# The normalised x of a gated layer: its scaling on ScalarE in place of GpSimd, in four slots of each chunk

## The chip, the cores and the metric

The kernel runs on one core of a Trainium2 chip. The metric is the device time of one execution in microseconds; what is compared is the median of several executions. The engines are named as the profile names them: PE is TensorE (matmuls), PEld its weight loads, DVE is VectorE, ACT is ScalarE, POOL is GpSimd, SP the engine that issues the DMAs.

## What is computed

x has the shape 4 x 2048 x 512. Each row is normalised to xn; one branch is a linear recurrence over the 2048 steps (q, k, v, a 128 x 128 memory M), the other a quantised feed-forward layer on the rows of xn with its own normalisation inside; the second, through a silu, gates the first.

```python
xn = (x - mean(x)) / sqrt(var(x) + 1e-5)

q, k, v = xn @ Wq.T, xn @ Wk.T, xn @ Wv.T
M_new = 0.99 * M + v_t.T @ k_t / b ;  r_t = q_t @ M.T
s = (r @ Wo.T) * sigmoid(gate)

h = (xn - mean(xn)) * rsqrt(var(xn) + 1e-5) * ln_gamma + ln_beta
y = silu(h @ dequant(fc1_q, fc1_scales) + fc1_bias)        # 512 -> 2048
z = y @ dequant(fc2_q, fc2_scales) + fc2_bias              # 2048 -> 512
g = silu(xn + 0.5 * z)
out = x + s * g
```

The change concerns the xn in `xn + 0.5 * z`: it is made again from x, late in the work on a chunk, as x times a scale of its row plus a shift of its row.

## The kernel before

The 2048 steps are cut into 16 chunks of 128 steps; with a batch of 4 that is four tiles of 128 rows by 512 columns a chunk (i from 0 to 3). Every engine runs the same hand-written loop of slots, 64 a chunk and 36 more at the end; what an engine does in slot e of a chunk is fixed by tables of slot numbers at the head of the file, and inside a slot by the order of the `if` lines in that engine's loop. Each engine works its own list strictly in order; semaphores tie the lists together.

In each slot TensorE does one step of fc1 (two matmuls of 128x512, L491) and one step of fc2 (two more, L509), and in some slots a side job of the recurrence: kv in slots 1, 13, 25, 37, q in slot 3, and for each tile kt, scores, read and wo at 4, 7, 11 and 14 slots after its kv, and a transposition (`turn`) in slots 52, 54, 57 and 60. The fc1 sum of a block J of 128 columns is built in four steps g, two slots apart. After each of the first three ScalarE multiplies the PSUM bank by a ratio (`rescale`, L638), and the next step waits for that; after the fourth it makes the silu (L645), and the first step of block J + 2, which uses the same bank, waits for that. Two blocks are worked in turn, so a rescale or silu of slot G is waited for by TensorE in slot G + 2, for the silus of even blocks as well. VectorE then splits y into two halves of 16 bits (`y_high` L760, `y_low` L765), which fc2 reads some slots later, and rescales the fc2 sum after each step (L774).

ScalarE also does the copies of the recurrence out of PSUM: `kv_copy` L610, `q_copy` L602, `kt_copy` L616, `r_copy` L621, `s_copy` L632, and, behind each `turn`, `g_high` L584 and `h_whole` L593. GpSimd splits h (L1073, L1077), makes the row statistics (L1038 to L1061) and normalises the next chunk's tiles (L1021).

A chunk is finished while the next one runs. In slots 8 to 11 of the next chunk VectorE puts z of the four tiles into `z_rows` (L779). GpSimd has made xn ready for it: `prepare` in slots 0, 3, 15 and 18 (`PREPARE_AT`) multiplies x by the row's scale and adds its shift (L1103), into one of the two buffers of `xz`, and then adds half of the fc2 bias to it in place (L1106). `add_z` in slots 13, 14, 17 and 20 (`ADD_AT`) adds it to `z_rows` (L1111). ScalarE makes the silu of that, `gate_silu` in slots 17, 19, 21 and 29 (`GATE_AT`, L664), and GpSimd multiplies by s and adds x, `output` in slots 18, 22, 26 and 30 (`OUT_AT`, L1117, L1120); SP stores the tile and loads the next x into its row of `x_again`. As `xz` has two buffers, the pieces for tiles 2 and 3 wait for the `add_z` of tiles 0 and 1. The last chunk is finished in the tail; its four `prepare` steps stand in its own slots 44, 46, 48 and 50 (`LAST_PREPARE_AT`) and write to `g_rows`, which is free then.

In the first chunk ScalarE uses the `xz` buffers for another purpose: it widens the fc2 weights there (`q2_widen`, L656), an activation with a scale and a shift from SBUF to SBUF.

Of the kernel before, what the change touches and what calls it, by code (L numbers as in the profile page):

```python
# [10 lines left out]
ALU = mybir.AluOpType  # L11
ACT = mybir.ActivationFunctionType
# [18 lines left out]
STEPS = 64  # L31
# [8 lines left out]
Q_AT = 3  # L40

Q_LAG, K_LAG, V_LAG, KT_LAG, R_LAG, S_LAG, GHIGH_LAG, HFULL_LAG = 1, 1, 2, 1, 1, 1, 1, 2
GATE_AT = (17, 19, 21, 29)

STATS_AT, MOMENTS_AT = (0, 1, 2, 3), (5, 6)
FIRST_STATS_AT, FIRST_MOMENTS_AT = (18, 20, 22, 24), (26, 27)
# [1 line left out]

HSPLIT_LAG = 3
NORMALISE_AT = (36, 38, 40, 42)  # L50
PREPARE_AT, ROWS_AT, FIRST_ROWS_AT = (0, 3, 15, 18), 7, 28

LAST_PREPARE_AT = (44, 46, 48, 50)
ADD_AT, OUT_AT = (13, 14, 17, 20), (18, 22, 26, 30)

Q1_AT = tuple(3 + 3 * n for n in range(FB // 2))
RATIO2_AT, TOP_Q2_AT, Q2_SCALE_AT = 6, (0, 1, 3, 5), 8
# [15 lines left out]
def build(nc, x, wqkv, wo, gate, m0, q1, q2, b2, params, out):  # L73
# [27 lines left out]
    def finishing(G, at, last_at):  # L101

        c, e = divmod(G, STEPS)
        if c == NCH:
            at = last_at
        return (c - 1, at.index(e)) if c > 0 and e in at else None

    def fc1_step(G):

        start = G if G % 2 == 0 else G - 5  # L110
        if start < 0:
            return None
        J, g = 2 * (start // 8) + G % 2, start % 8 // 2
        return (J, g) if J < NJ else None
# [20 lines left out]
    with ctx:  # L135
# [435 lines left out]
        def _(act):  # L571
# [16 lines left out]
            def h_whole(c, k, bank):  # L588
                if c == 0:
                    act.wait_ge(h_scales, 1)  # L590
                    act.wait_ge(turn_done, k + 1)
                wait(act, h_done, 4 * c + k - 1)
                act.activation(h_full[:, k % 2, :], bank[:], ACT.Identity,  # L593
                               bias=beta_s[:, k:k + 1], scale=gamma_s[:, k:k + 1]).then_inc(h_full_done, 1)
# [53 lines left out]
            def q2_widen(n):  # L648
# [4 lines left out]
                if n % 4 == 0:  # L653
# [2 lines left out]
                act.activation(wide[:, n % 2, :], q2_in_sb[:, n, :], ACT.Identity, bias=q2_shift[:, 0:1],  # L656
                               scale=up_q2).then_inc(q2_wide, 1)

            def gate_silu(c, i):
                if c < NCH - 1:  # L660
                    act.wait_ge(z_sum, NT * c + i + 1)
                else:
                    act.wait_ge(z_sum_last, i + 1)
                act.activation(z_rows[:, i, :], z_rows[:, i, :], ACT.Silu).then_inc(z_silu, 1)  # L664
# [31 lines left out]
            act.wait_ge(s1_scaled, 1)  # L696

            for G in range(SLOTS):
                if at := fc1_step(G):
                    if at[1] < KC - 1:  # L700
                        rescale(*at)
                    else:
                        silu(at[0])
                if G in Q1_AT:
                    if G == Q1_AT[0]:
                        act.wait_ge(q1_ready, 1)
                    q1_piece(FB // 2 + Q1_AT.index(G), up_q1, q1_shift[:, 0:1])
                if G in Q2_AT:
                    q2_widen(Q2_AT.index(G))
                if at := job_behind(G, Q_LAG, "q"):  # L710
                    q_copy(*at, side[JOB_BANK[G - Q_LAG]])
                if at := job_behind(G, K_LAG, "kv"):
                    kv_copy(*at, 0, side[JOB_BANK[G - K_LAG]])
                if at := job_behind(G, V_LAG, "kv"):
                    kv_copy(*at, 1, side[JOB_BANK[G - V_LAG]])
                if at := job_behind(G, KT_LAG, "kt"):
                    kt_copy(*at, side[JOB_BANK[G - KT_LAG]])
                if at := job_behind(G, R_LAG, "read"):
                    r_copy(*at, side[JOB_BANK[G - R_LAG]])
                if at := job_behind(G, S_LAG, "wo"):  # L720
                    s_copy(*at, side[JOB_BANK[G - S_LAG]])
                if at := job_behind(G, GHIGH_LAG, "turn"):
                    g_high(*at, side[JOB_BANK[G - GHIGH_LAG]])
                if at := job_behind(G, HFULL_LAG, "turn"):
                    h_whole(*at, side[JOB_BANK[G - HFULL_LAG]])
                if at := finishing(G, GATE_AT, LAST_GATE_AT):
                    gate_silu(*at)

# [279 lines left out]
        def _(pool):  # L1008
# [75 lines left out]

            def prepare(c, i):

                n = NT * c + i
                if c == 0 and i == 0:
                    pool.wait_ge(b2_halved, 1)
                if i == 0:  # L1090
                    pool.wait_ge(rows_done, c + 1)
                pool.wait_ge(x_again_in[i], 64 * (c + 1))
                to = xz[:, i % 2, :]
                if c == NCH - 1:
                    to = last_xz[:, i, :]
                    if i == 0:

                        pool.wait_ge(turn_done, KC * NCH)
                elif i >= 2:
                    pool.wait_ge(z_sum, NT * c + i - 1)  # L1100
                elif c > 0:
                    pool.wait_ge(z_sum, NT * (c - 1) + i + 3)
                pool.tensor_scalar(to, x_again[:, i, :], rs[:, c % 3, i:i + 1], nmr[:, c % 3, i:i + 1],  # L1103
                                   ALU.mult, ALU.add).then_inc(xz_scaled, 1)
                pool.wait_ge(xz_scaled, n + 1)
                pool.tensor_tensor(to, to, b2_half[:], ALU.add).then_inc(xz_done, 1)  # L1106

            def add_z(c, i):
# [96 lines left out]
```

## Time and profile before

| what | value |
|---|---|
| runs | 1252.54 us median of 3 (1252.32 to 1252.96) |
| the profiled execution | 1252.95 us, of which 1251.1 us are its span |
| granted TensorE clock, mean | 0.989 of full speed (2.4 GHz) |
| busy PE, DVE, ACT, POOL | 95%, 90%, 73%, 57% of the span |
| busy PEld | 49% of the span |
| chain that ended last | PE 78%, DVE 16%, issue 3%, ACT 1%, POOL 1% |

A row of the timeline has the start, the duration, engine, line and operation, what is written and read, and the count where neighbours were merged; in brackets stands the idle time of the engine before it, where there was any worth noting, and what ended it. Two neighbours on an engine may overlap: an instruction can be issued while the one before it still drains, so the distance from start to start is shorter than the duration. The middle chunk of the trace from which most rows are taken starts its slot 0 on TensorE at 562.53 us and its slot 16 at 584.53 us.

### The profile page before, as it was taken

How to read it: one execution, taken by the hardware profiler on the slowest of the kernel's cores; microseconds unless marked ns; L12 is line 12 of the kernel's file. 1: busy time of each engine (PE TensorE's matmuls, PEld its weight loads, DVE VectorE, ACT ScalarE, POOL GpSimd, SP SyncE). 2: the span in 40 equal slices, each digit the busy share in tenths (PEclk: the TensorE clock that was granted, in tenths of full speed). 3: DMA queues.
4: the chain of work that ended last, by engine and by line, in shares of the span. 5: the costliest groups of instructions: out<-in, count | busy, mean ns of one | idle time of the engine just before them, and what ended most of it. 6: DMA issues, size and time to landing. Idle time of an engine off the chain costs nothing.

```text
span 1251.1 us, 18966 instructions
## 1 busy us (share of the span) xinstructions
PE 1186.3 (95%) x6028; PEld 616.0 (49%) x6028; DVE 1124.8 (90%) x1965; ACT 913.8 (73%) x1590; POOL 711.4 (57%) x796
## 2 busy tenths in 40 slices
PE   2789999999999999999999999999999999999994
PEld 1344554545455554555555455454545545454551
DVE  7799899899998989999898989999898998999887
ACT  6588677777767777786777777777776777778673
POOL 6056737649273673927467383755837376492742
PEclk9799999999999999999999999999999999999997
DMA  9511030402103040120303113030210304020011
GB/s 332 178 42 34 20 83 1 102 1 57 45 9 94 1 102 1 43 60 1 102 1 81 22 30 73 1 101 1 67 35 18 85 1 101 1 55 13 24 46 35
DMA packets 41620, 65.68 MB, mean 52 GB/s; under 512 B 11696, under 2 KB 11952, under 8 KB 41008
## 3 DMA queue, kind: packets, MB, share of 16 engines
q1 hardware_dynamic: 41232, 64.36, 19.3%
q8 instruction: 51, 0.84, 0.3%
q14 instruction: 49, 0.40, 0.1%
q10 hardware_dynamic: 288, 0.08, 0.0%
HBM read 47.59 MB, written 16.81 MB: 51 GB/s over the span
## 4 chain that ended last, share of the span: by engine, by line
PE 78%; DVE 16%; issue 3%; ACT 1%; POOL 1%; DMA 1%; SPq 0%; DVEq 0%; ACTq 0%
PE blk L491 29%; PE blk L509 29%; PE side L451 7%; DVE blk L774 6%; PE side L476 4%; PE side L440 3%; DVE g_lo L744 3%; DVE y_split L765 2%; DVE y_split L760 2%; DVE tops L812 1%; PE side L469 1%; PE side L470 1%; PE side L468 1%; PE side L461 1%; PE side L427 1%
## 5 line engine op out<-in xcount | busy, mean ns | idle before, releaser
L774 DVE TENSOR_TENSOR blk<-blk,ratio_rows 128x512 f32<-128x512 f32 x960 | 649.3, 692 | 108.7 <-PE blk L509 97.9
L638 ACT ACTIVATE blk<-blk,ratio 128x512 f32<-128x512 f32 x768 | 508.2, 670 | 249.8 <-PE blk L491 240.2
L509 PE MATMUL blk<-w_sb,y_split 128*128 128x512 f16 x2048 | 609.0, 379 | 10.9 <-DVE y_split L765 8.1
L491 PE MATMUL blk<-h_split,q_sb 128*128 128x512 f16 x2048 | 612.8, 381 | 5.1 <-ACT blk L638 3.1
L509 PEld LDWEIGHTS blk<-w_sb,y_split 128*128 128x128 f16 x2048 | 197.1, 98 | 262.6 <-DVE blk L774 20.3
L491 PEld LDWEIGHTS blk<-h_split,q_sb 128*128 128x128 f16 x2048 | 192.9, 98 | 218.1 <-issue 36.8
L645 ACT ACTIVATE y_full<-blk,par,last 128x512 f32<-128x512 f32 x256 | 201.8, 788 | 55.0 <-PE blk L491 54.5
L1073 POOL CAST h_split<-h_full 128x512 f16<-128x512 f32 x64 | 41.0, 641 | 320.1 <-ACT h_full L593 320.0
L765 DVE SCALAR_TENSOR_TENSOR y_split<-y_full,up,y_split 128x512 f16<-128x512 f32 x256 | 214.8, 839 | 0.0
L760 DVE TENSOR_SCALAR y_split<-y_full,up 128x512 f16<-128x512 f32 x256 | 150.2, 587 | 0.0
L1117 POOL TENSOR_TENSOR z_rows<-z_rows,s_rows 128x512 f32<-128x512 f32 x62 | 93.3, 1504 | 36.2 <-ACT z_rows L664 36.2
L1106 POOL TENSOR_TENSOR xz<-xz,b_half 128x512 f32<-128x512 f32 x60 | 90.3, 1505 | 5.0
L1120 POOL TENSOR_TENSOR z_rows<-z_rows,x_again 128x512 f32<-128x512 f32 x62 | 87.5, 1411 | 4.9
L1111 POOL TENSOR_TENSOR z_rows<-z_rows,xz 128x512 f32<-128x512 f32 x60 | 82.7, 1387 | 7.9 <-DVE z_rows L779 6.7
L1077 POOL TENSOR_TENSOR h_split<-h_full,h_split 128x512 f16<-128x512 f32 x64 | 79.1, 1235 | 5.2
L451 PE MATMUL side<-wqkv_hi,g_hi 128*128 128x256 f16 x256 | 70.3, 274 | 7.2 <-DVE g_lo L744 4.8
L451 PE MATMUL side<-wqkv_lo,g_hi 128*128 128x256 f16 x256 | 70.3, 275 | 0.0
L451 PE MATMUL side<-wqkv_hi,g_lo 128*128 128x256 f16 x256 | 70.3, 275 | 0.0
L476 PE MATMUL side<-wo_sb,s_mask 128*128 128x512 f32 x128 | 65.5, 593 | 0.5 <-DVE mem_t L754 0.5
L1021 POOL TENSOR_SCALAR g_rows<-xt,gs,g_shift 128x512 f32<-128x512 f32 x64 | 54.7, 865 | 0.1
L1103 POOL TENSOR_SCALAR xz<-x_again,row_z 128x512 f32<-128x512 f32 x60 | 52.6, 876 | 0.0
L1038 POOL TENSOR_TENSOR v<-mv,row_const 128x4 f32<-128x4 f32 x16 | 3.2, 202 | 82.1 <-DVE mv L737 82.1
(154 smaller groups left out, 1152.4 us busy)
## 6 DMA issues: line engine op xcount, KB each, us to landing
xt<-in_x SPq DMA_DIRECT2D x64, 256.0 KB, 4.7
x_again<-in_x SPq DMA_DIRECT2D x256, 64.0 KB, 1.9
out<-z_rows SPq DMA_DIRECT2D x256, 64.0 KB, 1.7
w_sb<-in_q SPq DMA_DIRECT2D x4, 1024.0 KB, 13.8
ratio_rows<-ratio_dram SPq DMA_DIRECT2D x4, 1024.0 KB, 8.8
y_split<-in_q SPq DMA_DIRECT2D x1, 1024.0 KB, 10.2
h_split<-in_q SPq DMA_DIRECT2D x1, 1024.0 KB, 12.5
z_rows<-in_q SPq DMA_DIRECT2D x1, 1024.0 KB, 14.2
```

Source lines behind the costliest of these rows:

```text
L451: mm = pe.matmul(bank[:, 0:2 * M], a[:, k, rows], w[:, k, M:], start=(k == 0 and n == 0), stop=(k == KC - 1 and n == 2))
L476: pe.matmul(bank[:], r_t[:], wo_sb[:], start=True, stop=True).then_inc(wo_done, 1)
L491: mm = pe.matmul(blk[J % 2][:], q1_sb[:, g, j // 4, w, j % 4 * P:(j % 4 + 1) * P], a[:, c % 2, g, :], start=(g == 0 and n == 0), stop=(g = ...
L509: mm = pe.matmul(blk2[:, i, :], y[:, J % Y_RING, rows], w2_sb[:, j, part, :], start=(j == 0 and n == 0), stop=(j == FB - 1 and n == len(te ...
L638: act.activation(blk[J % 2][:], blk[J % 2][:], ACT.Copy, scale=ratio1[:, at:at + 1]).then_inc(blk_scaled, 1)
L645: act.activation(y_full[:, J % 2, :], blk[J % 2][:], ACT.Silu, bias=b1_c[:, j:j + 1], scale=last1[:, j:j + 1]).then_inc(silu_done, 1)
L760: dve.tensor_scalar(y_hi[:, J % Y_RING, :], y_full[:, J % 2, :], up_y, None, ALU.mult).then_inc(y_hi_done, 1)
L765: dve.scalar_tensor_tensor(y_lo[:, J % Y_RING, :], y_full[:, J % 2, :], up_y, y_hi[:, J % Y_RING, :], ALU.mult, ALU.subtract).then_inc(y_l ...
L774: dve.tensor_tensor(blk2[:, i, :], blk2[:, i, :], ratio2_rows[:, j, :], ALU.mult).then_inc(blk2_scaled, 1)
L1106: pool.tensor_tensor(to, to, b2_half[:], ALU.add).then_inc(xz_done, 1)
L1117: pool.tensor_tensor(z_rows[:, i, :], z_rows[:, i, :], s_rows[:, n % S_RING, :], ALU.mult).then_inc(z_mul, 1)
L1120: pool.tensor_tensor(z_rows[:, i, :], z_rows[:, i, :], x_again[:, i, :], ALU.add).then_inc(out_done, 1)
```

## The change

The first half of `prepare`, x times scale plus shift, goes from GpSimd to a new function of ScalarE, `normalise_again`, with the same waits, as one activation (Identity with scale and bias from `row_z`). It stands in slots 0, 3, 16 and 19 of the next chunk, and in slots 44, 46, 48 and 50 for the last chunk. GpSimd keeps the addition of half the bias, now in slots 1, 4, 17 and 20 (45, 47, 49, 51), and waits for ScalarE there. The third gate moves from slot 21 to 23; `add_z` of tiles 2 and 3 move from slots 17 and 20 to 18 and 22.

```diff
-GATE_AT = (17, 19, 21, 29)
+GATE_AT = (17, 19, 23, 29)
+XZ_AT, LAST_XZ_AT = (0, 3, 16, 19), (44, 46, 48, 50)
...
-PREPARE_AT, ROWS_AT, FIRST_ROWS_AT = (0, 3, 15, 18), 7, 28
-
-LAST_PREPARE_AT = (44, 46, 48, 50)
-ADD_AT, OUT_AT = (13, 14, 17, 20), (18, 22, 26, 30)
+PREPARE_AT, ROWS_AT, FIRST_ROWS_AT = (1, 4, 17, 20), 7, 28
+
+LAST_PREPARE_AT = (45, 47, 49, 51)
+ADD_AT, OUT_AT = (13, 14, 18, 22), (18, 22, 26, 30)
...
+            def normalise_again(c, i):
+
+                if i == 0:
+                    act.wait_ge(rows_done, c + 1)
+                act.wait_ge(x_again_in[i], 64 * (c + 1))
+                to = xz[:, i % 2, :]
+                if c == NCH - 1:
+                    to = last_xz[:, i, :]
+                    if i == 0:
+
+                        act.wait_ge(turn_done, KC * NCH)
+                elif i >= 2:
+                    act.wait_ge(z_sum, NT * c + i - 1)
+                elif c > 0:
+                    act.wait_ge(z_sum, NT * (c - 1) + i + 3)
+                else:
+
+                    act.wait_ge(q2_done, FB)
+                act.activation(to, x_again[:, i, :], ACT.Identity, bias=nmr[:, c % 3, i:i + 1],
+                               scale=rs[:, c % 3, i:i + 1]).then_inc(xz_scaled, 1)
...
+                if at := finishing(G, XZ_AT, ()):
+                    normalise_again(*at)
+                if c == NCH - 1 and e in LAST_XZ_AT:
+                    normalise_again(c, LAST_XZ_AT.index(e))
                 if at := finishing(G, GATE_AT, LAST_GATE_AT):
                     gate_silu(*at)
...
-                pool.tensor_scalar(to, x_again[:, i, :], rs[:, c % 3, i:i + 1], nmr[:, c % 3, i:i + 1],
-                                   ALU.mult, ALU.add).then_inc(xz_scaled, 1)
-                pool.wait_ge(xz_scaled, n + 1)
+                to = last_xz[:, i, :] if c == NCH - 1 else xz[:, i % 2, :]
+                pool.wait_ge(xz_scaled, NT * c + i + 1)
                 pool.tensor_tensor(to, to, b2_half[:], ALU.add).then_inc(xz_done, 1)
```

The new lines move the numbers of what follows: the rescale is L639 in the changed kernel, the silu L646, `s_copy` L633, `kt_copy` L617, the gate L686 and the new activation L678; on GpSimd the addition of the bias is L1118, `add_z` L1123, the two steps of the output L1129 and L1132.

ScalarE's list in slots 16 to 23 of a middle chunk, before (the numbers behind `blk` tell the two PSUM banks of fc1 apart):

```order
L632 ACTIVATE s_rows<-side1,row_c 128x512
L638 ACTIVATE blk1<-blk1,ratio1 128x512
L664 ACTIVATE z_rows<-z_rows 128x512
L638 ACTIVATE blk0<-blk0,ratio1 128x512
L616 ACTIVATE k_t<-side0 128x128
L645 ACTIVATE y_full<-blk1,par,last1 128x512
L664 ACTIVATE z_rows<-z_rows 128x512
L638 ACTIVATE blk0<-blk0,ratio1 128x512
L638 ACTIVATE blk1<-blk1,ratio1 128x512
L664 ACTIVATE z_rows<-z_rows 128x512
L645 ACTIVATE y_full<-blk0,par,last1 128x512
```

The same place in the changed kernel:

```order
L633 ACTIVATE s_rows<-side1,row_c 128x512
L678 ACTIVATE xz<-x_again,row_z 128x512
L639 ACTIVATE blk1<-blk1,ratio1 128x512
L686 ACTIVATE z_rows<-z_rows 128x512
L639 ACTIVATE blk0<-blk0,ratio1 128x512
L617 ACTIVATE k_t<-side0 128x128
L646 ACTIVATE y_full<-blk1,par,last1 128x512
L678 ACTIVATE xz<-x_again,row_z 128x512
L686 ACTIVATE z_rows<-z_rows 128x512
L639 ACTIVATE blk0<-blk0,ratio1 128x512
L639 ACTIVATE blk1<-blk1,ratio1 128x512
L646 ACTIVATE y_full<-blk0,par,last1 128x512
```

Two activations are new, one behind the `s_copy` and one behind the first silu; the third gate no longer stands ahead of the second silu.

GpSimd's list from slot 13 on, before, from the two `add_z` of tiles 0 and 1 to the first output and the last `add_z`:

```order
L1111 TENSOR_TENSOR z_rows<-z_rows,xz 128x512 x2
L1103 TENSOR_SCALAR xz<-x_again,row_z 128x512
L1106 TENSOR_TENSOR xz<-xz,b2_half 128x512
L1111 TENSOR_TENSOR z_rows<-z_rows,xz 128x512
L1103 TENSOR_SCALAR xz<-x_again,row_z 128x512
L1106 TENSOR_TENSOR xz<-xz,b2_half 128x512
L1117 TENSOR_TENSOR z_rows<-z_rows,s_rows 128x512
L1120 TENSOR_TENSOR z_rows<-z_rows,x_again 128x512
L1111 TENSOR_TENSOR z_rows<-z_rows,xz 128x512
```

The same place in the changed kernel:

```order
L1123 TENSOR_TENSOR z_rows<-z_rows,xz 128x512 x2
L1118 TENSOR_TENSOR xz<-xz,b2_half 128x512
L1123 TENSOR_TENSOR z_rows<-z_rows,xz 128x512
L1129 TENSOR_TENSOR z_rows<-z_rows,s_rows 128x512
L1132 TENSOR_TENSOR z_rows<-z_rows,x_again 128x512
L1118 TENSOR_TENSOR xz<-xz,b2_half 128x512
L1123 TENSOR_TENSOR z_rows<-z_rows,xz 128x512
```

The two multiplies are gone, and the second addition of the bias now stands behind the first output.

## Rows read from the trace of the kernel before

**Rows 1.** The page, busy us of each engine (share of the span) and instructions.

```profile
PE 1186.3 (95%) x6028; PEld 616.0 (49%) x6028; DVE 1124.8 (90%) x1965; ACT 913.8 (73%) x1590; POOL 711.4 (57%) x796
```

**Rows 2.** Windows, slots 16 to 24: length, busy PE PEld DVE ACT POOL, PEclk, DMA.

```profile
140.70:149.60 8.90, 8.90 (x47) 4.47 (x46) 8.54 (x15) 7.86 (x14) 8.58 (x8) 1.00 0.01 2
1176.20:1185.10 8.90, 8.90 (x46) 4.38 (x45) 8.69 (x15) 7.85 (x14) 6.76 (x5) 1.00 0.12 30
```

**Rows 3.** Timeline of ACT, slots 16 to 25: start us, us, engine, line.

```profile
585.75 0.68 ACT L632 ACTIVATE s_rows<-side,row_c 128x512 f32<-128x512 f32 x1
586.32 0.66 ACT L638 ACTIVATE blk<-blk,ratio 128x512 f32<-128x512 f32 x1
586.89 0.64 ACT L664 ACTIVATE z_rows<-z_rows 128x512 f32<-128x512 f32 x1
587.41 0.67 ACT L638 ACTIVATE blk<-blk,ratio 128x512 f32<-128x512 f32 x1
587.98 0.29 ACT L616 ACTIVATE k_t<-side 128x128 f32<-128x128 f32 x1
588.13 0.81 ACT L645 ACTIVATE y_full<-blk,par,last 128x512 f32<-128x512 f32 x1
588.80 0.66 ACT L664 ACTIVATE z_rows<-z_rows 128x512 f32<-128x512 f32 x1
589.32 1.27 ACT L638 ACTIVATE blk<-blk,ratio 128x512 f32<-128x512 f32 x2
590.46 0.67 ACT L664 ACTIVATE z_rows<-z_rows 128x512 f32<-128x512 f32 x1
590.98 0.82 ACT L645 ACTIVATE y_full<-blk,par,last 128x512 f32<-128x512 f32 x1
591.64 1.52 ACT L638 ACTIVATE blk<-blk,ratio 128x512 f32<-128x512 f32 x2
594.03 0.66 ACT L638 ACTIVATE blk<-blk,ratio 128x512 f32<-128x512 f32 x1 [0.87 <-PE blk L491]
```

**Rows 4.** Timeline of PE, the fc1 pairs of slots 19, 20, 22 and 24.

```profile
587.23 0.59 PE L491 MATMUL blk<-h_split,q_sb 128*128 128x512 f16 x2
...
588.13 0.61 PE L491 MATMUL blk<-h_split,q_sb 128*128 128x512 f16 x2
...
590.09 0.59 PE L491 MATMUL blk<-h_split,q_sb 128*128 128x512 f16 x2
...
591.86 0.60 PE L491 MATMUL blk<-h_split,q_sb 128*128 128x512 f16 x2
```

**Rows 5.** Groups of instructions: count | busy us, mean ns | idle before.

```profile
L1103 POOL TENSOR_SCALAR xz<-x_again,row_z 128x512 f32<-128x512 f32 x60 | 52.6, 876 | 0.0
L645 ACT ACT_TABLE_LOAD x1 | 1.3, 1283 | 0.0
```

**Rows 6.** Timeline of ACT in the first chunk, around one L656.

```profile
94.01 0.80 ACT L656 ACTIVATE xz<-w_sb,q_shift,up 128x512 f32<-128x512 int32 x1
94.71 0.68 ACT L632 ACTIVATE s_rows<-side,row_c 128x512 f32<-128x512 f32 x1
```

**Rows 7.** Timeline of ACT, the rescales of slots 2 and 4.

```profile
567.32 0.66 ACT L638 ACTIVATE blk<-blk,ratio 128x512 f32<-128x512 f32 x1 [2.01 <-PE blk L491]
...
571.64 0.66 ACT L638 ACTIVATE blk<-blk,ratio 128x512 f32<-128x512 f32 x1 [2.42 <-PE blk L491]
```

**Rows 8.** Timeline of POOL, the `add_z` of tiles 0 and 1.

```profile
582.85 2.50 POOL L1111 TENSOR_TENSOR z_rows<-z_rows,xz 128x512 f32<-128x512 f32 x2
```

**Rows 9.** Timeline of ACT, last chunk, slots 45 to 52: first and last idle.

```profile
1208.87 0.66 ACT L638 ACTIVATE blk<-blk,ratio 128x512 f32<-128x512 f32 x1 [0.42 <-PE blk L491]
...
1216.44 0.66 ACT L638 ACTIVATE blk<-blk,ratio 128x512 f32<-128x512 f32 x1 [0.94 <-PE blk L491]
```

**Rows 10.** Waits: who waited for whom, us in total, times, longest.

```profile
PE blk L509 <- DVE y_split L765: 8.1, 15, 1.7
PE side L451 <- DVE g_lo L744: 4.8, 14, 0.3
```

More of the change, by code:

```diff
@@ L698, in _ @@
             for G in range(SLOTS):
+                c, e = divmod(G, STEPS)
                 if at := fc1_step(G):
@@ L1085, in prepare @@
             def prepare(c, i):
-                n = NT * c + i
                 if c == 0 and i == 0:
                     pool.wait_ge(b2_halved, 1)
[L1090 to L1102, printed above, removed]
-                pool.tensor_scalar(to, x_again[:, i, :], rs[:, c % 3, i:i + 1], nmr[:, c % 3, i:i + 1],
-                                   ALU.mult, ALU.add).then_inc(xz_scaled, 1)
-                pool.wait_ge(xz_scaled, n + 1)
+                to = last_xz[:, i, :] if c == NCH - 1 else xz[:, i % 2, :]
+                pool.wait_ge(xz_scaled, NT * c + i + 1)
                 pool.tensor_tensor(to, to, b2_half[:], ALU.add).then_inc(xz_done, 1)
```

## The prediction

> **What bounds the kernel now.** I read the page's busy times first: TensorE is busy for 1186.3 of 1251.1 us, VectorE 1124.8, ScalarE 913.8, GpSimd 711.4 [rows 1]. By these shares the change looks free, work going from one engine with room to another with room. But a share is a mean over stages, so next I read the stage in which the moved work lands. A chunk is 64 slots; slots 16 to 24 of it are the stretch that [rows 2] shows for the first and for the last of the 15 chunks that finish a chunk before them. TensorE is busy in all 8.90 us of it, ScalarE in 7.86, at a granted clock of 1.00 of full speed (the 2.4 GHz level). The reader is to see that ScalarE there is not a 73% engine.
>
> Then the timeline of ScalarE in that stretch of one middle chunk [rows 3]. From the `s_copy` of slot 16 at 585.75 on, no row has an idle note until 594.03: the instructions follow each other at the distance in which they can be issued: 0.57 us after a rescale (586.32 to 586.89), 0.52 after a gate (586.89 to 587.41), 0.67 after a silu (588.13 to 588.80). The row at 589.32 holds the rescales of slots 20 and 21, that at 590.98 is the silu of slot 22.
>
> Who waits for them is read by laying TensorE's timeline beside it [rows 4]. Its fc1 pairs start at 587.23 (slot 19), 588.13 (slot 20), 590.09 (slot 22) and 591.86 (slot 24). The pair of slot 20 needs the rescale of slot 18, which starts at 587.41, takes 0.67 and so ends at 588.08, 0.05 before it. The pair of slot 24 needs the silu of slot 22, which ends at 590.98 + 0.82 = 591.80, 0.06 before. And the pair of slot 22 needs the rescale of slot 20, which at 0.67 ends at 589.99, 0.10 before. A slot with no side job takes 0.86 us on TensorE (0.43 a pair, fc1 and fc2), so slot 19 has lost 0.90 - 0.86 = 0.04 and slots 22 and 23 together 1.77 - 1.72 = 0.05. So in these eight slots TensorE paces the kernel, and ScalarE is behind it with next to nothing in hand. An instruction put into that row costs TensorE nearly its whole length.
>
> **The change, part by part.**
>
> What is removed: 60 GpSimd multiplies of 876 ns, and four of the last chunk [rows 5], 52.6 us and some 4 more. They are not on the path: what GpSimd hands on here goes to ScalarE's gates, and no gate of [rows 3] has idle time ahead of it, so none of them waits for GpSimd. I count the removal at zero.
>
> What is added: 64 ScalarE activations with a scale and a bias of one value a partition, SBUF to SBUF, 128x512. The trace of before has that form on integers, L656, in the first chunk: one starts at 94.01, takes 0.80, and the next instruction starts at 94.71 [rows 6]. What such a piece takes of an unbroken row is this distance, 0.70 us, and I take it; were a float input cheaper, the nearest lower row is the rescale's distance, 0.57 [rows 3], and that is the lower bound.
>
> Slots 0 and 3. The added work there starts at about 564.1 and 569.1. ScalarE's next rescales but one start at 567.32 after 2.01 us of idle time, and at 571.64 after 2.42 us, both ended by TensorE [rows 7], which has the long kv and q side jobs there. A piece of 0.70 us fits in each; the rescale of slot 1, which stands between, may start some 0.2 later, and its reader is behind the kv job. Cost: 0. Without these side jobs it would cost as much as in slots 16 and 19.
>
> Slots 16 and 19. The first stands between the `s_copy` and the rescale of slot 17, the second between the silu and the gate of slot 19. The third gate, which stood after the rescale of slot 21, moves to slot 23. Follow the rescale of slot 20: nothing is removed ahead of it and two pieces are added, so its start goes from 589.32 to 589.32 + 2 x 0.70 = 590.72; it ends at 591.39, and TensorE's slot 22 starts 0.05 after that, at 591.44, where it was 590.09. TensorE has stopped for 1.35 us by then, in pieces at slots 19, 20 and 22; nothing that it does in them delays ScalarE, whose row stays unbroken. Slots 22 and 23 take 0.86 each, and the silu of slot 22 is no longer late, since the gate ahead of it has gone; so slot 24 starts at 591.44 + 1.72 = 593.16 against 591.86. The loss is 1.30 us a chunk. The gate that was moved to slot 23 costs nothing: from 594.03 ScalarE idles 0.87 us and more before the next rescale [rows 3], behind the long side jobs of slots 24 and 25.
>
> The new waits of the two pieces. The one of slot 16 waits on ScalarE for the first `add_z` on GpSimd; behind it in ScalarE's row are rescales that TensorE needs. GpSimd does the first two from 582.85 in 2.50 us [rows 8], the first ends at about 584.1, and ScalarE comes to it at 586.32: 2.2 us in hand. The one of slot 19 needs the second, done at 585.35, and comes at 589.5. The inputs x_again were loaded a chunk earlier. Cost: 0; if GpSimd came over 2.2 us later, every further microsecond would be TensorE's.
>
> GpSimd's side. The addition of b2 now waits for ScalarE (from about 587.1 where it was 586.4), the third and fourth `add_z` go from slots 17 and 20 to 18 and 22. The third would end at some 590 and its gate now comes at 593.5; the fourth, behind the first output, at some 595.7, and its gate at over 601. Cost: 0.
>
> The last chunk. Its four pieces stand at slots 44, 46, 48 and 50. ScalarE has six idle pieces there, from 0.42 us at 1208.87 to 0.94 us at 1216.44 [rows 9], 2.83 us together, for 4 x 0.70 = 2.80. Most of the readers are behind a long job, so a late rescale there is not yet a late matmul. Cost: 0, at most 1 us once.
>
> **The sum.** 15 chunks x 1.30 = 19.5 us. The profiled execution took 1252.95 us (1251.1 of span and 1.85 around it), 0.41 above the median of 1252.54. So 1272.45 beside the profiled time, and 1272.0 beside the median. Bounds: with 0.57 a piece the rescale of slot 20 ends at 591.13, slot 22 starts at 591.18, slot 24 at 592.90: 1.04 a chunk, 15.6 in all. What VectorE makes of the shift is not in any row: its second y piece is read by TensorE's fc2 of slot 24 and moves with the silu of slot 19. That TensorE waits for it too is seen at the turn of the chunks, 8.1 us in 15 waits [rows 10], 0.54 each. I let half of one such wait bound it on both sides: given back, 1.04 - 0.27 = 0.77 a chunk or 11.6 in all; lost as well, 1.57 a chunk, with the 1 us of the last chunk 24.6 in all. Beside the median that is 1264 to 1277.
>
> The Trainium skill, Perfetto Trace Analysis, section Identifying the Most-Contended Engine, says to take the engine with the highest occupancy as the bottleneck. By the whole span's occupancy ScalarE would go from 73% to about 77% and stay far from the bound, and the sum would be zero; the trace of slots 16 to 24 disagrees, with 7.86 of 8.90 us and no idle row; its section Optimization Strategy does say that the most-contended engine can change from regime to regime.
>
> **The rivals.**
>
> No change: the whole-span reading, 1252.5. ScalarE has some 337 us without work, and 45 us more would fit if any lag could be caught up before a reader comes. For it: slots 0, 3 and the last chunk, as above. Against: readers in slots 19 to 24 that come 0.05 to 0.10 us after the writer. 4 in 100. That the change does not do what it says is not open: the orders show both engines' rows moved.
>
> Faster: if VectorE is held up by GpSimd's work beside it, less of that lets it be early at the turn of the chunk, where TensorE waits 8.1 us for the y piece and 4.8 for g_lo [rows 10]. Place: slots 0 and 1; price: all of it, 12.9 us or 0.86 a chunk, 1239.6 at the best. It decides the sign only if the two pieces at 16 and 19 cost under 0.86 us a chunk together. Against it: the GpSimd work that stands ahead of these waits is the split of h, which stays; the multiplies that go are behind them, or forty slots earlier, and VectorE idles in between. 3 in 100.
>
> Slower by more: ScalarE waits for GpSimd's first `add_z` in slot 16. Place: the 2.2 us in hand of [rows 8]; decides from there on. At 1 us past it, 15 us on top, 1287. Against: nothing ahead of that addition is changed. 6 in 100.
>
> A table load: the added function would have to be loaded in place of the silu's, and the silu's again after it. A load takes 1.28 us, and there is one at the first silu and no other among 256 [rows 5]. With two for each piece at slots 16 and 19, 15 x 2 x 2.57 = 77 us on top of the 19.5: 1349. Against: h_full is made by the same function among the silus, and brings no load. Under 1 in 100. The Trainium skill, ScalarE: Activation LUTs, section Table sets: the hidden batching unit, has it that a switch to another set costs a load but that cheap functions are in every set; the trace agrees on the second.
>
> **How the numbers follow.** The forecast, 11.6 to 24.6 us slower, gets 84 in 100; slower by more 7 (with the table load); slower by less than 11.6 but by over 0.2% (2.5 us, about what a measurement of this kernel can tell from no change) 2; within 0.2%, 4; faster, 3. Range 1264 to 1277, which leaves out 16 in 100. Faster 0.03, same 0.04, slower 0.93.
>
> **What would show each step.** In the changed profile the chunk's period grows by 1.30 us, and all of it between slots 16 and 24: there TensorE waits for ScalarE's rescale at slots 19, 20 and 22, for about 0.5, 0.2 and 0.7 us. ScalarE's busy time grows by 45 to 51 us, GpSimd's falls by some 56. The added instruction takes about 0.80 us. ScalarE's rescales after slots 0 and 3 start as before to 0.2 us. Wrong would be: ScalarE idle ahead of the new instruction at slot 16 (it waits for GpSimd), TensorE's new waits put down to VectorE, the loss at slots 0 to 4, or the turn of the chunk shorter than before.

## The result

The changed kernel takes 1271.58 us in the median of 4 runs (1271.04 to 1271.92), the kernel before 1252.75 beside it (1252.32 to 1253.61): 18.8 us more, a ratio of 1.0146 with the 95% interval 1.0134 to 1.0158. The prediction was 1272.0, in a range of 1264 to 1277. The profiled execution has a span of 1269.8 us at a granted clock of 0.992.

The page's busy times after the change, to be read against [rows 1]:

```profile
PE 1189.6 (94%) x6028; PEld 617.4 (49%) x6028; DVE 1132.0 (89%) x1965; ACT 958.0 (75%) x1654; POOL 637.2 (50%) x732
```

ScalarE has taken on 44.2 us, GpSimd has lost 74.2, and the kernel is slower. By shares ScalarE has only gone from 73% to 75%, and TensorE's own share has gone down. The stage tells more. Below are the windows of the first and the last chunk that finish another, from slot 16 to the start of slot 25 (columns as in [rows 2]); the same stretch was 8.87 us long before and is 10.2 now:

```profile
141.20:151.40 10.20, 9.29 (x46) 4.46 (x45) 9.14 (x16) 9.36 (x16) 8.10 (x7) 1.00 0.08 19
1193.60:1203.80 10.20, 9.29 (x47) 4.47 (x46) 8.51 (x16) 9.36 (x16) 7.29 (x6) 1.00 0.09 22
```

TensorE is no longer busy throughout: 9.29 of 10.20, at the full granted clock as before (1.00). ScalarE is busy for 9.36. This is its timeline in the same middle chunk as [rows 3], slots 16 to 22, with the first rescale that waits again at the end:

```profile
593.45 0.68 ACT L633 ACTIVATE s_rows<-side,row_c 128x512 f32<-128x512 f32 x1
594.01 0.81 ACT L678 ACTIVATE xz<-x_again,row_z 128x512 f32<-128x512 f32 x1
594.72 0.66 ACT L639 ACTIVATE blk<-blk,ratio 128x512 f32<-128x512 f32 x1
595.29 0.63 ACT L686 ACTIVATE z_rows<-z_rows 128x512 f32<-128x512 f32 x1
595.81 0.66 ACT L639 ACTIVATE blk<-blk,ratio 128x512 f32<-128x512 f32 x1
596.38 0.29 ACT L617 ACTIVATE k_t<-side 128x128 f32<-128x128 f32 x1
596.54 0.80 ACT L646 ACTIVATE y_full<-blk,par,last 128x512 f32<-128x512 f32 x1
597.20 0.84 ACT L678 ACTIVATE xz<-x_again,row_z 128x512 f32<-128x512 f32 x1
597.90 0.65 ACT L686 ACTIVATE z_rows<-z_rows 128x512 f32<-128x512 f32 x1
598.42 1.26 ACT L639 ACTIVATE blk<-blk,ratio 128x512 f32<-128x512 f32 x2
...
603.06 0.66 ACT L639 ACTIVATE blk<-blk,ratio 128x512 f32<-128x512 f32 x1 [0.64 <-PE blk L492]
```

No idle note, as before, and two more instructions in the row: the first takes 0.71 us of it (594.01 to 594.72), the second 0.70 (597.20 to 597.90). Neither waited for GpSimd. TensorE beside it, as in [rows 4] but with slot 18 ahead, so slots 18, 19, 20, 22 and 24:

```profile
594.07 0.59 PE L492 MATMUL blk<-h_split,q_sb 128*128 128x512 f16 x2
...
595.43 0.60 PE L492 MATMUL blk<-h_split,q_sb 128*128 128x512 f16 x2 [0.34 <-ACT blk L639]
...
596.53 0.61 PE L492 MATMUL blk<-h_split,q_sb 128*128 128x512 f16 x2
...
599.16 0.61 PE L492 MATMUL blk<-h_split,q_sb 128*128 128x512 f16 x2 [0.51 <-ACT blk L639]
...
600.90 0.60 PE L492 MATMUL blk<-h_split,q_sb 128*128 128x512 f16 x2
```

Slot 18 lasts 1.36 us in place of 0.86, slot 19 1.10 in place of 0.90, slot 21 1.54 in place of 0.86, and the two notes name ScalarE's rescale. Slot 20's pair has no note, but the rescale that it needs (595.81, 0.66 us) ends 0.06 us before it. A note is shorter than what its slot lost: a pair counts as busy for 0.59 us, while the next pair can start 0.43 us after it, so the first 0.16 us of a stop do not show as idle (0.50 lost against 0.34 noted, 0.67 against 0.51). From slot 19 to slot 24 it is 5.47 us where it was 4.63 in [rows 4], and slot 18 has its 0.50 before that.

The groups of the new activation and of two GpSimd steps:

```profile
L678 ACT ACTIVATE xz<-x_again,row_z 128x512 f32<-128x512 f32 x60 | 49.5, 824 | 0.0
...
L1129 POOL TENSOR_TENSOR z_rows<-z_rows,s_rows 128x512 f32<-128x512 f32 x62 | 89.4, 1442 | 38.2 <-ACT z_rows L686 38.2
L1118 POOL TENSOR_TENSOR xz<-xz,b_half 128x512 f32<-128x512 f32 x60 | 82.8, 1380 | 87.6 <-ACT xz L678 87.6
```

Two waits of TensorE, for ScalarE's rescale and for VectorE's y at the turn of the chunk [rows 10] (us in total, times, longest):

```profile
PE blk L492 <- ACT blk L639: 15.9, 38, 0.9
...
PE blk L510 <- DVE y_split L792: 8.1, 15, 1.7
```

In the kernel before, the first of them was:

```profile
PE blk L491 <- ACT blk L638: 3.1, 8, 0.9
```

The 30 new waits for a rescale are two a chunk; the waits for y at the turn of the chunk are what they were.

Over a whole chunk the traces differ in five slots: 18 (+0.50), 19 (+0.19), 21 (+0.67), 23 (-0.04) and 32 (-0.11 or -0.12), and by under 0.02 in any other. From slot 16 to slot 24 that is 8.67 us in place of 7.33, 1.34 more; with slot 32 the period goes from 73.97 to 75.17, 1.20 more. 14 such periods make 16.8 of the 18.7 us of span; the rest lies in the first chunk, the last one and the start.

### The profile page after: what moved, and what is told of

The parts are those of the page before. It is cut to its first block, busy times and chain, and to the rows that moved or that the text cites. A ratio compares the mean times of both kernels' runs of the same rounds, so it can differ in the third digit from the quotient of the medians.

```text
span 1269.8 us, 18968 instructions
## 1 busy us (share of the span) xinstructions
PE 1189.6 (94%) x6028; PEld 617.4 (49%) x6028; DVE 1132.0 (89%) x1965; ACT 958.0 (75%) x1654; POOL 637.2 (50%) x732
## 4 chain that ended last, share of the span: by engine, by line
PE 69%; DVE 16%; ACT 7%; issue 5%; DMA 1%; POOL 1%; SPq 0%; ACTq 0%; DVEq 0%
PE blk L492 26%; PE blk L510 25%; PE side L452 6%; DVE blk L801 6%; PE side L477 4%; PE side L441 3%; DVE g_lo L771 3%; DVE y_split L792 2%; DVE y_split L787 2%; ACT xz L678 2%; ACT blk L639 2%; DVE tops L839 1%; PE side L470 1%; PE side L471 1%; PE side L469 1%
## 5 line engine op out<-in xcount | busy, mean ns | idle before, releaser
L639 ACT ACTIVATE blk<-blk,ratio 128x512 f32<-128x512 f32 x768 | 507.2, 669 | 222.6 <-PE blk L492 214.0
L646 ACT ACTIVATE y_full<-blk,par,last 128x512 f32<-128x512 f32 x256 | 200.7, 784 | 56.2 <-PE blk L492 53.8
L792 DVE SCALAR_TENSOR_TENSOR y_split<-y_full,up,y_split 128x512 f16<-128x512 f32 x256 | 209.8, 819 | 0.0
L787 DVE TENSOR_SCALAR y_split<-y_full,up 128x512 f16<-128x512 f32 x256 | 160.8, 628 | 0.0
L1118 POOL TENSOR_TENSOR xz<-xz,b_half 128x512 f32<-128x512 f32 x60 | 82.8, 1380 | 87.6 <-ACT xz L678 87.6
L1129 POOL TENSOR_TENSOR z_rows<-z_rows,s_rows 128x512 f32<-128x512 f32 x62 | 89.4, 1442 | 38.2 <-ACT z_rows L686 38.2
L1132 POOL TENSOR_TENSOR z_rows<-z_rows,x_again 128x512 f32<-128x512 f32 x62 | 83.9, 1352 | 4.9
L1123 POOL TENSOR_TENSOR z_rows<-z_rows,xz 128x512 f32<-128x512 f32 x60 | 79.4, 1332 | 7.9 <-DVE z_rows L806 5.5
L678 ACT ACTIVATE xz<-x_again,row_z 128x512 f32<-128x512 f32 x60 | 49.5, 824 | 0.0
L594 ACT ACTIVATE h_full<-side,beta_s,gamma_s 128x512 f32<-128x512 f32 x60 | 48.9, 814 | 0.0
```

Of the source, the lines that this page charges most:

```text
L639: act.activation(blk[J % 2][:], blk[J % 2][:], ACT.Copy, scale=ratio1[:, at:at + 1]).then_inc(blk_scaled, 1)
L646: act.activation(y_full[:, J % 2, :], blk[J % 2][:], ACT.Silu, bias=b1_c[:, j:j + 1], scale=last1[:, j:j + 1]).then_inc(silu_done, 1)
L787: dve.tensor_scalar(y_hi[:, J % Y_RING, :], y_full[:, J % 2, :], up_y, None, ALU.mult).then_inc(y_hi_done, 1)
L792: dve.scalar_tensor_tensor(y_lo[:, J % Y_RING, :], y_full[:, J % 2, :], up_y, y_hi[:, J % Y_RING, :], ALU.mult, ALU.subtract).then_inc(y_l ...
L1129: pool.tensor_tensor(z_rows[:, i, :], z_rows[:, i, :], s_rows[:, n % S_RING, :], ALU.mult).then_inc(z_mul, 1)
L1132: pool.tensor_tensor(z_rows[:, i, :], z_rows[:, i, :], x_again[:, i, :], ALU.add).then_inc(out_done, 1)
```

## The experiments

The theory: an added piece costs what it delays an unbroken row of ScalarE behind which TensorE waits, so slots 16 and 19 cost all of it and the other places nothing. The rivals: each piece costs a share of its own, wherever it stands; ScalarE waits for GpSimd; or the moved gates and additions are the cause.

### Which of the pieces cost

Only the pieces of slots 0 and 3 stay on ScalarE. The other pieces go back to GpSimd, and the gates and additions of tiles 2 and 3 to their old slots. The edit is against the changed kernel, and `...` stands for what is left out:

```diff
...
-                if at := finishing(G, XZ_AT, ()):
+                if (at := finishing(G, XZ_AT, ())) and at[1] < 2:
                     normalise_again(*at)
...
```

> Only the pieces of slots 0 and 3 go to ScalarE (tiles 0 and 1 of each chunk); tiles 2 and 3 and the last chunk's four stay on GpSimd in their old slots, as do the gates. Theory (a piece costs what it delays an unbroken row, and slots 0 and 3 lie under TensorE's kv and q jobs): the time of the kernel before, within 1 us, 30 more activations for nothing. Rival (each of the 60 pieces costs the same share of the 18.8 us): 9.4 us slower than before, 1262.

Measured: 1253.31 us against 1253.15 for the kernel before, ratio 1.0001 (0.9992 to 1.0010). Thirty activations cost nothing that can be measured. TensorE's waits for the rescale are the 3.1 us in 8 of the kernel before:

```profile
PE blk L492 <- ACT blk L639: 3.1, 8, 0.9
```

Why is seen in the changed kernel's own timeline of ScalarE at slots 0 to 4, beside [rows 7]:

```profile
571.80 0.84 ACT L678 ACTIVATE xz<-x_again,row_z 128x512 f32<-128x512 f32 x1
...
575.02 0.66 ACT L639 ACTIVATE blk<-blk,ratio 128x512 f32<-128x512 f32 x1 [1.83 <-PE blk L492]
...
576.81 0.81 ACT L678 ACTIVATE xz<-x_again,row_z 128x512 f32<-128x512 f32 x1
579.34 0.66 ACT L639 ACTIVATE blk<-blk,ratio 128x512 f32<-128x512 f32 x1 [1.72 <-PE blk L492]
```

The idle times before the rescales of slots 2 and 4 have shrunk from 2.01 and 2.42 us to 1.83 and 1.72, and they are still ended by TensorE.

Only slots 16 and 19, with the change's gates and additions; the other pieces go back to GpSimd (against the changed kernel, cut as above):

```diff
...
-                if at := finishing(G, XZ_AT, ()):
+                if (at := finishing(G, XZ_AT, ())) and at[1] >= 2:
                     normalise_again(*at)
-                if c == NCH - 1 and e in LAST_XZ_AT:
-                    normalise_again(c, LAST_XZ_AT.index(e))
...
```

> Only the pieces of slots 16 and 19 go to ScalarE (tiles 2 and 3), with the gates and additions in the slots of the change; tiles 0 and 1 and the last chunk's stay on GpSimd. Theory: all of the loss is here, 1271 to 1273. Rival (same share for each piece): 1262. Rival (the loss comes from the last chunk or the first slots): the time of before.

Measured: 1271.78 us, ratio 1.0151 (1.0136 to 1.0167). All of the loss is here, and in the trace it stands in the same slots with the same sizes as in the changed kernel. The rival of an equal share for each piece is out with either run.

### Is it the length of the piece

The changed kernel with the new activation on 256 of the 512 columns; it leaves the other half of xn unscaled:

```diff
-                act.activation(to, x_again[:, i, :], ACT.Identity, bias=nmr[:, c % 3, i:i + 1],
+                act.activation(to[:, 0:H // 2], x_again[:, i, 0:H // 2], ACT.Identity, bias=nmr[:, c % 3, i:i + 1],
```

> The changed kernel with the new activation on the first 256 of 512 columns (the other half of xn is left unscaled). Theory: the piece takes 0.49 in place of 0.70 us of the row, so the two delay it by 0.98 in place of 1.41, 0.43 less a chunk: 6.4 us faster than the changed kernel, 1265. Rival (a wait for GpSimd or for a semaphore, of whatever length the piece is): the changed kernel's time, 1271.6.

Measured: 1264.58 us, ratio 1.0093 (1.0077 to 1.0109), 7.0 us under the changed kernel's median. ScalarE's timeline at slot 16:

```profile
591.43 0.60 ACT L678 ACTIVATE xz<-x_again,row_z 128x256 f32<-128x256 f32 x1
591.92 0.66 ACT L639 ACTIVATE blk<-blk,ratio 128x512 f32<-128x512 f32 x1
```

The piece takes 0.49 us of the row, 0.22 less, and slots 18 and 21 each last 0.21 less. The cost goes with the length of what stands in the row. A wait for GpSimd would not shrink with it. Slot 19 keeps its 1.10 us: it has become the distance between two rescales in ScalarE's row with a gate between them (594.72 to 595.81 above, 1.09), and that the shorter piece leaves as it is.

### Is it the gates, the additions or GpSimd's order

The changed kernel with the third gate back in slot 21:

```diff
-GATE_AT = (17, 19, 23, 29)
+GATE_AT = (17, 19, 21, 29)
```

> The changed kernel with the third gate back in slot 21. Theory: it stands ahead of the silu of slot 22 again, which then ends about 0.05 to 0.1 us behind what TensorE could have: 15 x 0.09 = 1.3 us slower than the changed kernel, some 1273. Rival (a gate in that row costs its whole 0.52 us): 7.8 us slower, 1279. Rival (the move of the gate is itself what costs): faster than the changed kernel.

Measured: 1271.98 us, ratio 1.0156 (1.0142 to 1.0170). In time this is not told apart from the changed kernel (1.0134 to 1.0158). In the trace slot 23 is 0.92 us long in place of 0.86, and no other slot differs by 0.02: 0.9 us over the run, in the direction expected. So the move of the gate neither costs the 18.8 us nor saves much.

The kernel before with the moved slots alone, the multiplication staying on GpSimd:

```diff
-GATE_AT = (17, 19, 21, 29)
+GATE_AT = (17, 19, 23, 29)
-PREPARE_AT, ROWS_AT, FIRST_ROWS_AT = (0, 3, 15, 18), 7, 28
+PREPARE_AT, ROWS_AT, FIRST_ROWS_AT = (1, 4, 17, 20), 7, 28
-LAST_PREPARE_AT = (44, 46, 48, 50)
-ADD_AT, OUT_AT = (13, 14, 17, 20), (18, 22, 26, 30)
+LAST_PREPARE_AT = (45, 47, 49, 51)
+ADD_AT, OUT_AT = (13, 14, 18, 22), (18, 22, 26, 30)
```

> The kernel before with the moved slots alone: the third gate in slot 23, the two additions in slots 18 and 22, GpSimd's steps in slots 1, 4, 17 and 20 (45, 47, 49, 51 in the last chunk); the multiplication stays on GpSimd. Theory: the slots cost nothing, and the silu of slot 22 is on time: 0 to 1.5 us faster than before, 1251 to 1253. Rival (the loss comes from GpSimd's later additions and gates): 5 us slower or more.

Measured: 1258.80 us, ratio 1.0046 (1.0032 to 1.0060). This was missed: 5.6 us slower, where I had counted the moves at nothing. The trace puts 0.50 us a chunk on slot 24, where TensorE waits for VectorE's y: 13.8 us in 30 waits over the run, twice as often as in [rows 10]. Slots 23 and 32 give 0.04 and 0.12 of it back, so the period is 74.31 us against 73.97.

```profile
PE blk L509 <- DVE y_split L765: 13.8, 30, 1.7
```

First the kernel before at this place, GpSimd and then VectorE (`y_high` of slot 20):

```profile
589.41 0.77 POOL L1103 TENSOR_SCALAR xz<-x_again,row_z 128x512 f32<-128x512 f32 x1
```

```profile
589.81 0.64 DVE L760 TENSOR_SCALAR y_split<-y_full,up 128x512 f16<-128x512 f32 x1
```

Then the run with the moved slots alone, where the first output has come to stand ahead of the last piece of xn: GpSimd, VectorE's `y_high` and `y_low`, and TensorE's fc2 of slot 24:

```profile
591.56 1.27 POOL L1117 TENSOR_TENSOR z_rows<-z_rows,s_rows 128x512 f32<-128x512 f32 x1
```

```profile
591.99 1.12 DVE L760 TENSOR_SCALAR y_split<-y_full,up 128x512 f16<-128x512 f32 x1
...
593.83 0.96 DVE L765 SCALAR_TENSOR_TENSOR y_split<-y_full,up,y_split 128x512 f16<-128x512 f32 x1
```

```profile
594.94 0.59 PE L509 MATMUL blk<-w_sb,y_split 128*128 128x512 f16 x2 [0.35 <-DVE y_split L765]
```

In both kernels `y_high` ends nearly the same time after the GpSimd instruction that it began beside: 590.45 against 590.18, 0.27 us; 593.11 against 592.83, 0.28 us. Where GpSimd has nothing running it takes 0.47 or 0.48 in every trace. So its length follows what is left of GpSimd's instruction, and a multiply of 0.77 us in that place is kinder than a two-input one of 1.27. The Trainium skill, SBUF — State Buffer, section SBUF: two separate sides, says that VectorE and GpSimd share a pair of ports as an exclusive lock: against a VectorE instruction in a 2-port mode, or with two inputs from SBUF, whichever of the two starts first has the pair for its whole length, and the other blocks. These rows agree in that `y_high` ends 0.27 and 0.28 us behind GpSimd; in which mode it works no run here shows.

Was it the gate? The kernel before with the third gate in slot 23 and nothing else:

```diff
-GATE_AT = (17, 19, 21, 29)
+GATE_AT = (17, 19, 23, 29)
```

> The kernel before with the third gate in slot 23 and nothing else. Formed after the run with the moved slots alone came out 5.6 us slower, where 0 to 1.5 faster was expected: in that run GpSimd's first output stands ahead of its last piece of xn, a two-input instruction that runs beside VectorE's y_high of slot 20, which takes 1.12 in place of 0.64 us, and TensorE waits 0.5 us for y in slot 24. Theory: with GpSimd's order as before that wait is not there, 1251.5 to 1253. Rival (the gate in slot 23 is what costs): 1258.

Measured: 1252.76 us against 1252.56, ratio 1.0002 (0.9993 to 1.0012). Slot 24 has no new wait. Slot 23 is 0.04 us shorter and slot 32 0.03 longer. So it is not the gate but the moved steps of GpSimd that cost the 5.6 us; by the rows above it is the output that stands ahead. A run that moves this output alone was not made.

Is that cost part of the 18.8 us as well? The changed kernel with the first output behind the last addition of b2:

```diff
-ADD_AT, OUT_AT = (13, 14, 18, 22), (18, 22, 26, 30)
+ADD_AT, OUT_AT = (13, 14, 18, 22), (21, 22, 26, 30)
```

> The changed kernel with GpSimd's first output behind its last addition of b2 (slot 21 in place of 18), as it stood before the change. Theory: the later y of slot 24, which cost 0.5 us a chunk in the run with the moved slots alone, is hidden behind the 1.36 us that TensorE has by then lost to ScalarE: the changed kernel's time, 1271 to 1272. Rival (GpSimd's order is part of the 18.8 us): 5 us faster, 1266.

Measured: 1275.95 us, ratio 1.0181 (1.0165 to 1.0196). Theory and rival both missed: it is 4.4 us slower than the changed kernel. Slots 18 to 21 are unchanged, but slot 24 lasts 0.15 and slot 27 0.13 us longer. GpSimd and VectorE at slot 20 there:

```profile
599.96 1.26 POOL L1118 TENSOR_TENSOR xz<-xz,b_half 128x512 f32<-128x512 f32 x1 [0.60 <-ACT xz L678]
```

```profile
600.06 1.45 DVE L787 TENSOR_SCALAR y_split<-y_full,up 128x512 f16<-128x512 f32 x1
```

The addition of b2, let go by ScalarE, now begins 0.10 us ahead of `y_high` and holds it for its whole length: it ends at 601.51, 0.29 after GpSimd, and takes 1.45 us. In the changed kernel it takes 0.82 at this place. There `y_low`, and TensorE's fc2 of slot 24 that reads it, are:

```profile
599.75 0.95 DVE L792 SCALAR_TENSOR_TENSOR y_split<-y_full,up,y_split 128x512 f16<-128x512 f32 x1
```

```profile
601.33 0.59 PE L510 MATMUL blk<-w_sb,y_split 128*128 128x512 f16 x2
```

TensorE comes to this y 0.63 us after it is ready (600.70). The 0.63 more of `y_high` use that up, and TensorE starts 0.15 after the end of a y that it waits for (594.79 to 594.94 above): that is the 0.15 of slot 24. What makes slot 27 longer was not followed up. So the cost of the moved slots at slot 24 is hidden in the changed kernel, and a change in GpSimd's order alone brings a part of it out.

### Where the pieces could stand

The changed kernel with the late pieces where ScalarE idles, slots 24 and 25, and the gates behind them:

```diff
-GATE_AT = (17, 19, 23, 29)
-XZ_AT, LAST_XZ_AT = (0, 3, 16, 19), (44, 46, 48, 50)
+GATE_AT = (17, 19, 27, 37)
+XZ_AT, LAST_XZ_AT = (0, 3, 24, 25), (44, 46, 48, 50)
-PREPARE_AT, ROWS_AT, FIRST_ROWS_AT = (1, 4, 17, 20), 7, 28
+PREPARE_AT, ROWS_AT, FIRST_ROWS_AT = (1, 4, 24, 26), 7, 28
-ADD_AT, OUT_AT = (13, 14, 18, 22), (18, 22, 26, 30)
+ADD_AT, OUT_AT = (13, 14, 25, 27), (18, 22, 28, 38)
```

> The changed kernel with the two late pieces moved from slots 16 and 19 to 24 and 25, where ScalarE idles (0.87 and 1.32 us in the kernel before), GpSimd's steps behind them, and the third and fourth gates in slots 27 and 37. Theory (a piece costs what it delays an unbroken row): no rescale is late, and the stops of slots 23, 31 and 32 (0.05, 0.15, 0.13 us) go: 1248 to 1251, no slower than before. VectorE against GpSimd, as in the run with the moved slots alone, may take 0.3 a chunk of it back: up to 1253. Rival (ScalarE's load as such, 45 us more): 1265 or more.

Measured: 1257.73 us, ratio 1.0040 (1.0026 to 1.0055), above what was expected. The ScalarE part came out: TensorE's waits for a rescale are 3.1 us in 8 again, slot 23 is 0.04 and slot 31 0.16 shorter than before the change. But slot 32 is 0.45 longer and slot 24 0.07, and the waits for y are 30:

```profile
PE blk L510 <- DVE y_split L792: 14.5, 30, 1.7
```

GpSimd and VectorE ahead of slot 32:

```profile
601.05 1.27 POOL L1129 TENSOR_TENSOR z_rows<-z_rows,s_rows 128x512 f32<-128x512 f32 x1
```

```profile
601.52 1.08 DVE L787 TENSOR_SCALAR y_split<-y_full,up 128x512 f16<-128x512 f32 x1
```

`y_high` ends at 602.60, 0.28 after GpSimd: the same collision, one y later.

The gates moved so on the kernel before, with the multiplication on GpSimd:

```diff
-GATE_AT = (17, 19, 21, 29)
+GATE_AT = (17, 19, 27, 37)
-ADD_AT, OUT_AT = (13, 14, 17, 20), (18, 22, 26, 30)
+ADD_AT, OUT_AT = (13, 14, 17, 20), (18, 22, 28, 38)
```

> The kernel before, all four multiplications on GpSimd in their old slots, with the third and fourth gates in slots 27 and 37 and their outputs in 28 and 38. Theory: ScalarE's row loses 0.52 us in slots 21 and 29, so the stops of slots 23, 31 and 32 shrink: 1 to 5 us faster than before, 1248 to 1252. If it comes out as the run with the late pieces in slots 24 and 25, then it is the gates and not the place of the multiplication that helps there.

Measured: 1252.88 us against 1252.56, ratio 1.0002 (0.9992 to 1.0011), a little above the 1248 to 1252 expected. Slots 23 and 31 give 0.20 us a chunk and slot 32 takes 0.19 of it back. With the pieces and additions in slots 24 to 27 as well, slot 32 took 0.45, so the gates alone do not make all of that loss.

If it is GpSimd's work beside `y_high` that slot 32 pays for, that work has to start later. GpSimd is not paced by slots but by what it waits for, so the gates are put into slots 36 and 37 (against the run with the pieces in slots 24 and 25):

```diff
-GATE_AT = (17, 19, 27, 37)
+GATE_AT = (17, 19, 36, 37)
-ADD_AT, OUT_AT = (13, 14, 25, 27), (18, 22, 28, 38)
+ADD_AT, OUT_AT = (13, 14, 25, 27), (18, 22, 37, 38)
```

> The late pieces on ScalarE in slots 24 and 25 as before, but the third and fourth gates in slots 36 and 37 and their outputs in 37 and 38, so that GpSimd has nothing two-input to do while VectorE makes the y that slot 32 reads (in the run with the gates in 27 and 37 y_high took 1.08 us, ending 0.28 us after GpSimd's instruction beside it, and slot 32 lost 0.45 us). Theory: slot 32 takes 1.08 to 1.10 us, slots 23 and 31 lose nothing: 0.25 a chunk less than before, 1248 to 1250. Rival (the 0.45 us is not GpSimd's doing): 1257, as in that run.

Measured: 1249.67 us against 1253.09, ratio 0.9971 (0.9961 to 0.9982): faster than both kernels. ScalarE in slots 24 to 26 of its trace, then GpSimd and VectorE ahead of slot 32:

```profile
592.41 0.80 ACT L678 ACTIVATE xz<-x_again,row_z 128x512 f32<-128x512 f32 x1
593.44 0.66 ACT L639 ACTIVATE blk<-blk,ratio 128x512 f32<-128x512 f32 x1 [0.23 <-PE blk L492]
...
594.18 0.81 ACT L678 ACTIVATE xz<-x_again,row_z 128x512 f32<-128x512 f32 x1
595.61 0.66 ACT L639 ACTIVATE blk<-blk,ratio 128x512 f32<-128x512 f32 x1 [0.62 <-PE blk L492]
```

```profile
598.78 0.77 POOL L1048 TENSOR_SCALAR g_rows<-xt,gs,g_shift 128x512 f32<-128x512 f32 x1
```

```profile
599.24 0.60 DVE L787 TENSOR_SCALAR y_split<-y_full,up 128x512 f16<-128x512 f32 x1
...
600.35 0.74 DVE L792 SCALAR_TENSOR_TENSOR y_split<-y_full,up,y_split 128x512 f16<-128x512 f32 x1
```

The two pieces fill idle time and some is left behind each. `y_high` meets only a short multiply (it ends 0.29 after that), and `y_low` is alone: 0.74 us. Slots 23, 31 and 32 are 0.04, 0.16 and 0.13 shorter than in the kernel before, slot 24 is 0.07 longer; the period is 73.71 against 73.97.

The kernel before with the same late gates, the multiplication on GpSimd:

```diff
-GATE_AT = (17, 19, 21, 29)
+GATE_AT = (17, 19, 36, 37)
-ADD_AT, OUT_AT = (13, 14, 17, 20), (18, 22, 26, 30)
+ADD_AT, OUT_AT = (13, 14, 17, 20), (18, 22, 37, 38)
```

> The kernel before, all multiplications on GpSimd, with the third and fourth gates in slots 36 and 37 and their outputs in 37 and 38. Theory: as the run with the pieces on ScalarE in slots 24 and 25, 1247 to 1250, because GpSimd's multiplication is off the path: what helps is when the gates and outputs run. Rival (GpSimd's work must shrink for it): the time of before, 1252.6.

Measured: 1250.26 us, ratio 0.9977 (0.9968 to 0.9986). As expected, or 0.3 above: nearly all of the gain needs no move of the multiplication. The periods are 73.67 here and 73.71 there. What the move gives is at one place: in the last chunk slot 48 is 1.65 us longer here than in the kernel before, where TensorE waits 1.49 us for a y; in the run with ScalarE making the four pieces of that chunk it is not. The two ratios overlap, so the difference in time is not established.

## Why the prediction was right

**The bound read in the stage.** Right. By the shares of [rows 1] there was room on ScalarE; by [rows 3] and [rows 4] there was none between slots 16 and 24. The half-width run and the run with slots 16 and 19 alone show the cost in that row, and by its length.

**The size of the piece.** Right: 0.70 was taken from the integer form of [rows 6], 0.71 and 0.70 were measured; 0.80 expected for its own duration, 0.824 in the mean. ScalarE's busy time grew by 44.2 us, a little under the 45 to 51 expected.

**The walk to slot 24.** Right: 1.30 us expected, 1.34 measured (0.50 + 0.19 + 0.67 - 0.04 = 1.32 in the four slots that differ by more than 0.02); the three stops were expected at about 0.5, 0.2 and 0.7. The silu of slot 22 came off the path as the prediction had it.

**Slots 0 and 3, the last chunk, the new waits.** Right at zero, each. The run with slots 0 and 3 alone shows the first. No new activation has idle time ahead of it, so none waited for GpSimd. In the last chunk nothing is longer after slot 25.

**"Cost: 0" for the moved gates and additions.** Right to about 0.1 us a chunk as a term of this sum, and wrong as a reading. By themselves the moves cost 5.6 us, through VectorE: the first output, moved ahead in GpSimd's list, holds `y_high` up. The prediction looked only at whether what GpSimd hands on comes late, and did not ask whom GpSimd's instructions disturb. In the changed kernel, by its trace, the y of slot 24 is ready 0.63 us ahead of TensorE, which has stopped for ScalarE by then. That the term came out is luck: what covers it is the stop that the second piece makes in slot 21 (0.67 us), behind the silu of that y.

**What VectorE makes of the shift.** Bounded at 0.27 on either side; measured 0.12 a chunk to the good, at slot 32, which is the most of why 1.34 a chunk in the stretch became 1.20 in the period. The bound held, but the prediction had no reason for this place. `y_high` of slot 28, whose y slot 32 reads, before and then after:

```profile
599.83 0.78 DVE L760 TENSOR_SCALAR y_split<-y_full,up 128x512 f16<-128x512 f32 x1
```

```profile
608.86 0.48 DVE L787 TENSOR_SCALAR y_split<-y_full,up 128x512 f16<-128x512 f32 x1
```

The run with the moved slots alone has the same 0.12 at slot 32 and the one with the gate alone does not, so it comes with the moves of GpSimd's steps and not with the multiplication. That the time met the forecast within 0.4 us is in part luck: this gain went one way, and 0.04 us a chunk more in the stretch and 0.4 us more in the start the other.

**GpSimd's busy time.** Mis-sized: a fall of 56 us was expected and it is 74. The multiplies make 56.6 of it; the rest is that GpSimd's two-input instructions on `xz` and `z_rows` got shorter, the addition of b2 from 1505 to 1380 ns and the first step of the output from 1504 to 1442 in the mean. The prediction took these as fixed. That they are shorter because they meet VectorE less often would fit the collisions above, but it is not shown.

**The rivals.** No change: refuted, and with it the whole-span reading. Faster through VectorE at the turn of the chunk: the waits there are 8.1 us in 15 before and after. Slower through a wait for GpSimd: no such wait. A table load: ScalarE's count of instructions has grown by 64, the new activations, and by nothing else.

## What to carry to other kernels

Before work is moved to an engine with a low share, lay that engine's timeline beside its reader's at the very slot: if its rows have no idle note and the reader comes 0.05 us after the writer, every added instruction costs nearly its full distance from start to start, and a few slots on, behind a long job of the reader, the same instruction is free. A moved instruction must be asked three things: who waits for what it makes, what stands behind it on its engine, and whom it disturbs while it runs. When the place is freely chosen, choose it by the idle notes of the trace, then look again: here the better place for ScalarE first brought out a collision between GpSimd and VectorE.

## What the runs showed of the hardware

VectorE's `y_high` (128x512, f32 to f16, one input) takes 0.47 us alone and ends 0.27 to 0.29 us after the GpSimd instruction that was running when it began, in the five places shown above (GpSimd instructions of 0.77 to 1.27 us): it took 0.60 to 1.45 us there. The size of such a collision is thus set by what is left of GpSimd's instruction.

It is not so in every case. The change itself turns a collision round early in each chunk. Before, the multiply that goes away begins just ahead of a `y_high`:

```profile
195.25 1.06 POOL L1103 TENSOR_SCALAR xz<-x_again,row_z 128x512 f32<-128x512 f32 x1
```

```profile
195.28 0.48 DVE L760 TENSOR_SCALAR y_split<-y_full,up 128x512 f16<-128x512 f32 x1
```

After, the addition of b2 stands there in its place:

```profile
196.95 1.26 POOL L1118 TENSOR_TENSOR xz<-xz,b_half 128x512 f32<-128x512 f32 x1
```

```profile
197.00 1.49 DVE L787 TENSOR_SCALAR y_split<-y_full,up 128x512 f16<-128x512 f32 x1
```

In the first pair `y_high` is not held, although the multiply began 0.03 us ahead of it, and it is the multiply that is long (1.06 us, where it took 0.77 above). In the second pair `y_high` is three times as long. Whether this comes from the 0.02 us between the two cases or from the kind of GpSimd instruction is not shown. TensorE loses nothing by it: no slot from 0 to 17 differs by 0.02 us.

A periodic kernel is a good instrument: from the second chunk on the period repeats to 0.03 us or better inside one execution, so a change of 0.05 us in one slot can be read from a trace where the time of the whole run cannot show it.
